# Splitting a pair's products into two calls on TensorE, with the spread as two half-height row tiles

## The chip, the cores and the metric

The kernel runs on one NeuronCore of a Trainium2 chip. The metric is the device time of one execution in microseconds (us), lower is better.

## The reference

2048 samples, each with 200 goods of 32 numbers and one candidate of 32 numbers:

```
outer  = einsum('bi,bnj->bnij', candidate, goods)           # 32*32 per item
h1     = concat(candidate, goods, outer)                    # 2048 x 200 x 1088
act    = sigmoid(h1 @ W1 + b1)                              # 36 hidden
weight = act @ W2 + b2                                      # 2048 x 200 x 1
out    = sum(goods * weight, axis=1)                        # 2048 x 32
```

## The kernel before, in words

Since the candidate is fixed within a sample, `h1 @ W1` is `goods @ Wb + bias`, where `Wb` (32 x 36) and the bias depend on the sample alone. The start of the kernel (some 24 us) makes all the `Wb` into `wm` (32 hidden units) and `wxd` (the other four) and the biases. After that the kernel runs over 64 pairs.

A unit is four samples, one in each block of 32 partitions (the block is called r). A pair is eight units, numbered by s (0 or 1) and c (0 to 3). One DMA of 800 KB brings a pair's `goods`, seven slots deep. In an iteration of the main loop TensorE works, in this order, on three different pairs:

- `products(p)`: for s, r and c one 32x32 product of 200 columns into `z_ps`, bank r, columns of s, partitions of c. The trace shows two MATMULs for each float32 product, so 64 in a call. The r-th group of s = 0 first waits until ScalarE has read bank r for pair p - 1 (`act_done`). `z_done` goes up once for each r, in the s = 1 round.
- `spread(q, 0)` and `spread(q, 1)` for q = p - 3: bf16 products with a 0/1 matrix `pick` that spread the item weights of a unit over its 128 partitions, for two units a call into one bank `s_ps[f % 2]`. Each waits for VectorE to have pooled what that bank held (`pooled`).
- `row_sums(p - 1, 0..2)`: the product with W2 into `w_ps`, 24 MATMULs with 32 columns of weights, once all of pair p - 1 is through the sigmoid (`act_done`, `actx_done`).
- `products_x(p, 0..1)`: the four other hidden units, 16 MATMULs into `x_ps`.
- `spread(q, 2)` and `spread(q, 3)`.

ScalarE does, for each r, the sigmoids of s = 0 and s = 1 (`act`, L346; waits for `z_done`, counts `act_done` once for each r) and then `actx` (L351). VectorE pools two units for each spread call (`pool_units`, L383: multiply by `goods` and sum over the 200 items), and copies `w_ps` with the bias to `whole` (`keep`, L376). GpSimd splits `whole` into three bf16 parts, which stand in `stack` (L192 to L201), and every eighth pair lays out more of `wx` (L180). Each engine works through its own list in order; semaphores tie them. The goods load of pair p waits on `pooled` for pair p - 7.

Of the kernel before, what the change touches and what calls it, by code (L numbers as in the profile page):

```python
# [10 lines left out]
P = 128  # L11
B, N, K, H = 2048, 200, 32, 36
HM = 32
# [28 lines left out]
def build(nc, goods_t, cand_r, cand_u, w1_outer, small, pick, out_t):  # L42
    with ExitStack() as ctx:  # L43
# [17 lines left out]
        pick_sb = sb("pick_sb", [P, PAIR_U, P], BF16)  # L61
# [20 lines left out]
        w2m = consts[:, C_W2M:C_W2X].rearrange("p (s m) -> p s m", s=2)  # L82
        w2x = consts[:, C_W2X:C_B2].rearrange("p (r m) -> p r m", r=4)
# [88 lines left out]
        def _(pool):  # L172
# [17 lines left out]
            for q in range(PAIRS):  # L190
# [7 lines left out]
                if q >= 2:  # L198

                    pool.wait_ge(s_done, 4 * (q - 1))  # L200
# [7 lines left out]
        def _(pe):  # L208
# [35 lines left out]
            def products(p):  # L244
                pe.wait_ge(goods_loaded[p % G_SLOTS], 16 * (p // G_SLOTS + 1))
                for s in range(2):
                    for r in range(4):
                        if s == 0 and p >= 1:

                            pe.wait_ge(act_done, 4 * (p - 1) + r + 1)  # L250
                        for c in range(4):
                            u = PAIR_U * p + 4 * s + c
                            last = nc.tensor.matmul(z_ps[32 * c:32 * c + 32, r, N * s:N * s + N],  # L253
                                                    wm[32 * r:32 * r + 32, u // RUN, :, u % RUN],
                                                    goods[32 * r:32 * r + 32, p % G_SLOTS, 4 * s + c, :],
                                                    start=True, stop=True)
                        if s == 1:
                            last.then_inc(z_done, 1)
# [15 lines left out]
            def row_sums(p, step):  # L274
                if step == 0:
                    if p >= 1:

                        pe.wait_ge(w_kept, p)
                    pe.wait_ge(act_done, 4 * p + 4)
                if step == 2:  # L280
                    pe.wait_ge(actx_done, p + 1)
                for r in range(4):
                    if step < 2:
                        left, right = w2m[:, step, :], act[:, p % A_SLOTS, r, N * step:N * step + N]
                    else:
                        left, right = w2x[:, r, :], actx[:, p % A_SLOTS, :]
                    last = nc.tensor.matmul(w_ps[32 * r:32 * r + 32, 0:N], left, right,  # L287
                                            start=step == 0, stop=step == 2)
# [3 lines left out]
            def spread(q, f):  # L292
# [4 lines left out]
                if 4 * q + f >= 2:  # L297

                    pe.wait_ge(pooled, 4 * q + f - 1)
                for i in range(2):  # L300
                    v = 2 * f + i
                    last = nc.tensor.matmul(s_ps[f % 2][:, N * i:N * i + N], pick_sb[:, v, :], stack[:, q % 2, :],  # L302
                                            start=True, stop=True)
                last.then_inc(s_done, 1)

            for p in range(PAIRS + LAG):
                q = p - LAG
                if p < PAIRS:
                    products(p)
                if q >= 0:  # L310
                    spread(q, 0)
                    spread(q, 1)
# [3 lines left out]
                if p < PAIRS:  # L316
                    products_x(p, 0)
                    products_x(p, 1)
                if q >= 0:
                    spread(q, 2)  # L320
                    spread(q, 3)

        @block.scalar
        def _(sc):
# [14 lines left out]
            for p in range(PAIRS):  # L339
# [3 lines left out]
                for r in range(4):  # L343
                    sc.wait_ge(z_done, 4 * p + r + 1)
                    for s in range(2):
                        last = nc.scalar.activation(act[:, p % A_SLOTS, r, N * s:N * s + N],  # L346
                                                    z_ps[:, r, N * s:N * s + N], ACT.Sigmoid,
                                                    bias=bias[:, r, p, s:s + 1])
                    last.then_inc(act_done, 1)
# [109 lines left out]
```

## Time and profile before

| | us |
|---|---|
| median of 3 runs | 299.07 (298.53 to 303.03) |
| the profiled execution, its time | 298.97 |
| its span, first to last instruction | 297.0 |
| TensorE busy in the span | 281.6 |
| ScalarE, VectorE, GpSimd busy | 204.3, 198.4, 195.9 |
| mean granted TensorE clock | 0.989 of full |

Busy time counts a matmul from its start to its modelled end, and overlapping matmuls once. The work of one pair repeats 64 times, so the timeline of one pair in the middle, from one `products` to the next, is the thing to read.

### The profile page before, as it was taken

Reading aid. Unit: us, or ns where it says so; the run is one execution under the profiler, and the core shown is the slowest. Engines: PE = TensorE matmul, PEld = TensorE weight load, DVE = VectorE, ACT = ScalarE, POOL = GpSimd, SP = SyncE. Lnnn points to the kernel's source line nnn. Section 1 sums busy time; section 2 is a strip of 40 time slices with the busy share of each in tenths; the row PEclk is TensorE's granted clock in tenths of the full one; section 3 lists DMA queues with packets and bytes.
Section 4 is the critical chain, followed back from the end, with each engine's and each line's share of the span. In section 5 each row is a group of like instructions: output and inputs, shape, how many; then the busy total and the mean of one; then the engine's idle time right before and its main releaser. Section 6 shows DMA issues by size and latency. Waiting matters only on the chain.

```text
span 297.0 us, 17453 instructions
## 1 busy us (share of the span) xinstructions
PE 281.6 (95%) x7480; PEld 179.6 (60%) x7480; DVE 198.4 (67%) x1109; ACT 204.3 (69%) x596; POOL 195.9 (66%) x293
## 2 busy tenths in 40 slices
PE   1997999999999999999999999999999999999983
PEld 0333666666666666666666666665666666666641
DVE  0592176766776776767767677676776767767677
ACT  2495878767777677777777877777677776777730
POOL 9900686678666876677766867676676656766663
PEclk9997999999999999999999999999999999999997
DMA  7890036556766566665666656666566765657000
GB/s 254 333 421 25 4 115 210 183 181 216 223 218 191 173 228 214 219 215 153 214 211 225 212 173 204 211 221 227 143 210 211 229 224 152 206 210 222 8 2 9
DMA packets 10588, 55.69 MB, mean 188 GB/s; under 512 B 1168, under 2 KB 1936, under 8 KB 10384
## 3 DMA queue, kind: packets, MB, share of 16 engines
q1 hardware_dynamic: 10080, 54.01, 55.3%
q8 instruction: 59, 0.97, 1.3%
q10 hardware_dynamic: 432, 0.58, 0.5%
q14 instruction: 17, 0.14, 0.2%
HBM read 54.32 MB, written 0.26 MB: 184 GB/s over the span
## 4 chain that ended last, share of the span: by engine, by line
PE 89%; ACT 4%; DVE 3%; DMA 2%; issue 1%; POOL 0%; POOLq 0%; DVEq 0%
PE z_ps L253 28%; PE w_ps L287 26%; PE s_ps L302 19%; PE x_ps L269 15%; ACT wm L337 3%; DMA act<-w_outer 2%; DVE goods L383 2%; PE z_ps L220 1%; ACT act L346 1%; DVE wxd L363 1%; PE x_ps L220 1%; POOL mid L196 0%; POOLq L43 0%; DVE bias L366 0%; DVE whole L376 0%
## 5 line engine op out<-in xcount | busy, mean ns | idle before, releaser
L346 ACT ACTIVATE act<-z_ps,bias 128x200 f32<-128x200 f32 x512 | 169.7, 443 | 69.7 <-PE z_ps L253 69.7
L383 DVE CUSTOM_DVE_ANT_0 goods<-s_ps,goods 128x200 f32<-128x200 f32 x512 | 156.5, 363 | 64.4 <-PE s_ps L302 64.4
L192 POOL TENSOR_SCALAR top<-whole,consts 128x200 bf16<-128x200 f32 x64 | 50.1, 783 | 76.7 <-DVE whole L376 76.1
L253 PE MATMUL z_ps<-goods,wm 32*32 32x200 f32 x4096 | 90.0, 357 | 1.7 <-issue 1.6
L253 PEld LDWEIGHTS z_ps<-goods,wm 32*32 32x32 f32 x4096 | 59.5, 145 | 21.1 <-issue 13.8
L302 PE MATMUL s_ps<-stack,pick_sb 128*128 128x200 bf16 x512 | 67.2, 252 | 3.2 <-DVE out_stage L383 2.6
L302 PEld LDWEIGHTS s_ps<-stack,pick_sb 128*128 128x128 bf16 x512 | 36.3, 98 | 42.7 <-issue 22.4
L287 PE MATMUL w_ps<-act,consts 128*32 128x200 f32 x1024 | 58.4, 339 | 0.7 <-issue 0.6
L269 PE MATMUL x_ps<-goods,wx 128*32 128x200 f32 x1024 | 58.0, 337 | 0.0
L196 POOL TENSOR_SCALAR mid<-rest,consts 128x200 bf16<-128x200 f32 x64 | 50.1, 782 | 6.3
L383 DVE DVE_READ_ACCUMULATOR2_ANT out_stage<- 128x1 f32 x512 | 42.8, 84 | 0.0
L376 DVE TENSOR_SCALAR whole<-w_ps,consts 128x200 f32<-128x200 f32 x64 | 27.3, 426 | 21.8 <-PE w_ps L287 15.3
L269 PEld LDWEIGHTS x_ps<-goods,wx 128*32 128x32 f32 x1024 | 34.7, 110 | 11.2 <-issue 0.9
L201 POOL TENSOR_TENSOR stack<-rest,mid 128x200 bf16<-128x200 f32 x64 | 36.4, 568 | 5.3
L194 POOL TENSOR_TENSOR rest<-whole,top 128x200 f32<-128x200 f32 x64 | 36.3, 567 | 5.3
L287 PEld LDWEIGHTS w_ps<-act,consts 128*32 128x32 f32 x1024 | 27.0, 109 | 17.0 <-issue 12.0
L287 PE MATMUL w_ps<-actx,consts 128*32 128x200 f32 x512 | 35.6, 333 | 0.5 <-issue 0.4
L351 ACT ACTIVATE actx<-x_ps,biasx 128x200 f32<-128x200 f32 x64 | 30.1, 471 | 2.3 <-PE x_ps L269 2.2
L287 PEld LDWEIGHTS w_ps<-actx,consts 128*32 128x32 f32 x512 | 17.5, 110 | 6.9 <-issue 2.0
L220 PE MATMUL z_ps<-act 32*32 32x512 f32 x160 | 10.4, 724 | 6.2 <-DMA act<-w_outer 6.2
L180 POOL COPY wx<-wxd 32x256 f32<-32x256 f32 x32 | 12.6, 394 | 2.0
L173 POOL MEMSET wx<- 128x12288 f32 x1 | 10.3, 10342 | 0.3 <-POOLq L448 0.3
(28 smaller groups left out, 56.4 us busy)
## 6 DMA issues: line engine op xcount, KB each, us to landing
goods<-goods_t SPq DMA_DIRECT2D x64, 800.0 KB, 4.4
act<-cand_r SPq DMA_DIRECT2D x1, 1024.0 KB, 5.3
act<-cand_u SPq DMA_DIRECT2D x1, 256.0 KB, 6.0
pick_sb<-pick ACTq DMA_DIRECT2D x1, 256.0 KB, 6.1
out_t<-out_stage SPq DMA_DIRECT2D x4, 64.0 KB, 4.2
consts<-small ACTq DMA_DIRECT2D x1, 164.5 KB, 6.1
act<-w_outer ACTq DMA_DIRECT2D x1, 144.0 KB, 5.4
```

The lines of the kernel that those rows point to most:

```text
L192: nc.gpsimd.tensor_scalar(top[:, :], whole[:, q % 2, :], m1, None, ALU.mult).then_inc(part_step, 1)
L194: nc.gpsimd.tensor_tensor(rest[:, :], whole[:, q % 2, :], top[:, :], ALU.subtract).then_inc(part_step, 1)
L196: nc.gpsimd.tensor_scalar(mid[:, :], rest[:, :], m2, None, ALU.mult).then_inc(part_step, 1)
L201: nc.gpsimd.tensor_tensor(stack[:, q % 2, :], rest[:, :], mid[:, :], ALU.subtract).then_inc(part_step, 1)
L253: last = nc.tensor.matmul(z_ps[32 * c:32 * c + 32, r, N * s:N * s + N], wm[32 * r:32 * r + 32, u // RUN, :, u % RUN], goods[32 * r:32 * r ...
L269: last = nc.tensor.matmul(x_ps[32 * c:32 * c + 32, 0:N], left, goods[:, p % G_SLOTS, 4 * s + c, :], start=s == 0, stop=s == 1)
L287: last = nc.tensor.matmul(w_ps[32 * r:32 * r + 32, 0:N], left, right, start=step == 0, stop=step == 2)
L302: last = nc.tensor.matmul(s_ps[f % 2][:, N * i:N * i + N], pick_sb[:, v, :], stack[:, q % 2, :], start=True, stop=True)
L346: last = nc.scalar.activation(act[:, p % A_SLOTS, r, N * s:N * s + N], z_ps[:, r, N * s:N * s + N], ACT.Sigmoid, bias=bias[:, r, p, s:s + 1])
L351: nc.scalar.activation(actx[:, p % A_SLOTS, :], x_ps[:, 0:N], ACT.Sigmoid, bias=biasx[:, p:p + 1]).then_inc(actx_done, 1)
L376: nc.vector.tensor_scalar(whole[:, p % 2, :], w_ps[:, 0:N], b2, None, ALU.add).then_inc(w_kept, 1)
L383: last = nc.vector.tensor_tensor_reduce(goods[:, q % G_SLOTS, v, :], s_ps[f % 2][:, N * i:N * i + N], goods[:, q % G_SLOTS, v, :], 1.0, 0. ...
```

## The change

`products` takes s as an argument and does one round of 32 MATMULs; each round has its own waits and its own four counts of `z_done`, so ScalarE does the four sigmoids of s = 0, then `actx`, then the four of s = 1, and counts `act_done` after each. The r-th group of round s waits for ScalarE to have read bank r of the round before it; for s = 1 that is round 0 of the same pair.

The rows of `stack` are laid out anew: the lower 64 partitions hold the item weights of the units of s = 0, the upper 64 those of s = 1. A spread call uses 64 rows for each product, with the s = 0 ones into `s_ps[0]` and the s = 1 ones into `s_ps[1]`, and does four units; there are two calls to a pair instead of four. Each waits until all four units of the call before are pooled. `pick` has half the columns. The `act` slices and weights of `row_sums` change with the layout; its count of MATMULs doesn't. The order on TensorE becomes: products(p, 0), spread(q, 0), products_x(p, 0 and 1), products(p, 1), spread(q, 1), row_sums(p - 1). The number of goods transfers and their sizes, and SyncE's code, stay as they are.

```diff
             pe.wait_ge(wb_kept[0], KEPT_ALL)
             pe.wait_ge(wb_kept[1], KEPT_ALL)
 
-            def products(p):
-                pe.wait_ge(goods_loaded[p % G_SLOTS], 16 * (p // G_SLOTS + 1))
-                for s in range(2):
-                    for r in range(4):
-                        if s == 0 and p >= 1:
-
-                            pe.wait_ge(act_done, 4 * (p - 1) + r + 1)
-                        for c in range(4):
-                            u = PAIR_U * p + 4 * s + c
-                            last = nc.tensor.matmul(z_ps[32 * c:32 * c + 32, r, N * s:N * s + N],
-                                                    wm[32 * r:32 * r + 32, u // RUN, :, u % RUN],
-                                                    goods[32 * r:32 * r + 32, p % G_SLOTS, 4 * s + c, :],
-                                                    start=True, stop=True)
-                        if s == 1:
-                            last.then_inc(z_done, 1)
+            def products(p, s):
+                if s == 0:
+                    pe.wait_ge(goods_loaded[p % G_SLOTS], 16 * (p // G_SLOTS + 1))
+                for r in range(4):
+                    if 2 * p + s >= 1:
+
+                        pe.wait_ge(act_done, 4 * (2 * p + s - 1) + r + 1)
+                    for c in range(4):
+                        u = PAIR_U * p + 4 * s + c
+                        last = nc.tensor.matmul(z_ps[32 * c:32 * c + 32, r, N * s:N * s + N],
+                                                wm[32 * r:32 * r + 32, u // RUN, :, u % RUN],
+                                                goods[32 * r:32 * r + 32, p % G_SLOTS, 4 * s + c, :],
+                                                start=True, stop=True)
+                    last.then_inc(z_done, 1)
...
-                    pe.wait_ge(act_done, 4 * p + 4)
+                    pe.wait_ge(act_done, 8 * p + 8)
                 if step == 2:
                     pe.wait_ge(actx_done, p + 1)
-                for r in range(4):
+                for t in range(4):
+
                     if step < 2:
-                        left, right = w2m[:, step, :], act[:, p % A_SLOTS, r, N * step:N * step + N]
+                        first = N * (t // 2)
+                        left, right = w2m[:, step, :], act[:, p % A_SLOTS, 2 * (t % 2) + step, first:first + N]
                     else:
-                        left, right = w2x[:, r, :], actx[:, p % A_SLOTS, :]
-                    last = nc.tensor.matmul(w_ps[32 * r:32 * r + 32, 0:N], left, right,
+                        left, right = w2x[:, t, :], actx[:, p % A_SLOTS, :]
+                    last = nc.tensor.matmul(w_ps[32 * t:32 * t + 32, 0:N], left, right,
                                             start=step == 0, stop=step == 2)
                 if step == 2:
                     last.then_inc(w_done, 1)
...
-                if 4 * q + f >= 2:
-
-                    pe.wait_ge(pooled, 4 * q + f - 1)
+                if 2 * q + f >= 1:
+
+                    pe.wait_ge(pooled, 4 * q + 2 * f)
                 for i in range(2):
-                    v = 2 * f + i
-                    last = nc.tensor.matmul(s_ps[f % 2][:, N * i:N * i + N], pick_sb[:, v, :], stack[:, q % 2, :],
-                                            start=True, stop=True)
+                    for s in range(2):
+                        rows = slice(64 * s, 64 * s + 64)
+                        last = nc.tensor.matmul(s_ps[s][:, N * i:N * i + N], pick_sb[rows, 2 * f + i, :],
+                                                stack[rows, q % 2, :], start=True, stop=True)
                 last.then_inc(s_done, 1)
 
             for p in range(PAIRS + LAG):
                 q = p - LAG
                 if p < PAIRS:
-                    products(p)
+                    products(p, 0)
                 if q >= 0:
                     spread(q, 0)
+                if p < PAIRS:
+                    products_x(p, 0)
+                    products_x(p, 1)
+                    products(p, 1)
+                if q >= 0:
                     spread(q, 1)
                 if 1 <= p <= PAIRS:
                     for step in range(3):
                         row_sums(p - 1, step)
-                if p < PAIRS:
-                    products_x(p, 0)
-                    products_x(p, 1)
-                if q >= 0:
-                    spread(q, 2)
-                    spread(q, 3)
 
...
-                for r in range(4):
-                    sc.wait_ge(z_done, 4 * p + r + 1)
-                    for s in range(2):
-                        last = nc.scalar.activation(act[:, p % A_SLOTS, r, N * s:N * s + N],
-                                                    z_ps[:, r, N * s:N * s + N], ACT.Sigmoid,
-                                                    bias=bias[:, r, p, s:s + 1])
-                    last.then_inc(act_done, 1)
-                sc.wait_ge(x_done, p + 1)
-                nc.scalar.activation(actx[:, p % A_SLOTS, :], x_ps[:, 0:N], ACT.Sigmoid,
-                                     bias=biasx[:, p:p + 1]).then_inc(actx_done, 1)
+                for s in range(2):
+                    for r in range(4):
+                        sc.wait_ge(z_done, 4 * (2 * p + s) + r + 1)
+                        nc.scalar.activation(act[:, p % A_SLOTS, r, N * s:N * s + N],
+                                             z_ps[:, r, N * s:N * s + N], ACT.Sigmoid,
+                                             bias=bias[:, r, p, s:s + 1]).then_inc(act_done, 1)
+                    if s == 0:
+                        sc.wait_ge(x_done, p + 1)
+                        nc.scalar.activation(actx[:, p % A_SLOTS, :], x_ps[:, 0:N], ACT.Sigmoid,
+                                             bias=biasx[:, p:p + 1]).then_inc(actx_done, 1)
...
-                dve.wait_ge(s_done, 4 * q + f + 1)
-                for i in range(2):
-                    v = 2 * f + i
-                    u = PAIR_U * q + v
-                    last = nc.vector.tensor_tensor_reduce(
-                        goods[:, q % G_SLOTS, v, :], s_ps[f % 2][:, N * i:N * i + N], goods[:, q % G_SLOTS, v, :],
-                        1.0, 0.0, ALU.mult, ALU.add, out_stage[:, u:u + 1])
-                last.then_inc(pooled, 1)
+                dve.wait_ge(s_done, 2 * q + f + 1)
+                for s in range(2):
+                    for i in range(2):
+                        v = 4 * s + 2 * f + i
+                        u = PAIR_U * q + v
+                        last = nc.vector.tensor_tensor_reduce(
+                            goods[:, q % G_SLOTS, v, :], s_ps[s][:, N * i:N * i + N], goods[:, q % G_SLOTS, v, :],
+                            1.0, 0.0, ALU.mult, ALU.add, out_stage[:, u:u + 1])
+                    last.then_inc(pooled, 1)
...
-                if q >= 0:
-                    pool_units(q, 2)
-                    pool_units(q, 3)
...
-    pick = np.zeros((4, 32, PAIR_U, 4, 32), mybir.dt.np(BF16))
+
+    pick = np.zeros((2, 2, 32, 4, 4, 32), mybir.dt.np(BF16))
     for r in range(4):
+        half, e = divmod(r, 2)
+        for c in range(4):
+            three = slice(12 * e + 3 * c, 12 * e + 3 * c + 3)
+            w2m[c, :, e, three] = w2[:HM, None]
+            pick[:, half, three, c, r, :] = 1.0
+            masks[:, 12 * e + 3 * c + 1:12 * e + 3 * c + 3, 0] = 1.0
+            masks[:, 12 * e + 3 * c + 2, 1] = 1.0
+            for s in range(2):
+                w2x[c, s, r, :, 2 * s + half, three] = w2[HM:, None]
```

## Rows read from the trace of the kernel before

**Rows 1.** The page: busy time, then the chain that ended last by engine.
```profile
PE 281.6 (95%) x7480; PEld 179.6 (60%) x7480; DVE 198.4 (67%) x1109; ACT 204.3 (69%) x596; POOL 195.9 (66%) x293
...
PE 89%; ACT 4%; DVE 3%; DMA 2%; issue 1%; POOL 0%; POOLq 0%; DVEq 0%
```

**Rows 2.** The page's costliest groups: ScalarE's sigmoid of the products.
```profile
L346 ACT ACTIVATE act<-z_ps,bias 128x200 f32<-128x200 f32 x512 | 169.7, 443 | 69.7 <-PE z_ps L253 69.7
```

**Rows 3.** Timeline of one pair, TensorE; start us, us, engine line op tiles xcount.
```profile
149.94 1.38 PE L253 MATMUL z_ps<-goods,wm 32*32 32x200 f32 x64
...
151.26 0.52 PE L302 MATMUL s_ps<-stack,pick_sb 128*128 128x200 bf16 x4
...
151.70 0.88 PE L287 MATMUL w_ps<-act,consts 128*32 128x200 f32 x16
...
152.74 0.86 PE L269 MATMUL x_ps<-goods,wx 128*32 128x200 f32 x16
...
153.54 0.52 PE L302 MATMUL s_ps<-stack,pick_sb 128*128 128x200 bf16 x4
...
153.99 1.37 PE L253 MATMUL z_ps<-goods,wm 32*32 32x200 f32 x64
```

**Rows 4.** Timeline, TensorE, windows up to 150.04, 150.28 and 151.30 in one products call.
```profile
149.94 0.48 PE L253 MATMUL z_ps<-goods,wm 32*32 32x200 f32 x15
...
149.94 0.65 PE L253 MATMUL z_ps<-goods,wm 32*32 32x200 f32 x32
...
150.60 0.72 PE L253 MATMUL z_ps<-goods,wm 32*32 32x200 f32 x26
```

**Rows 5.** Timeline of the same pair, ScalarE.
```profile
151.22 2.65 ACT L346 ACTIVATE act<-z_ps,bias 128x200 f32<-128x200 f32 x8 [1.06 <-PE z_ps L253]
```

**Rows 6.** Timeline of an early pair: ScalarE, then TensorE's loads and matmuls.
```profile
31.32 0.78 ACT L346 ACTIVATE act<-z_ps,bias 128x200 f32<-128x200 f32 x2
...
31.67 1.66 PE L253 MATMUL z_ps<-goods,wm 32*32 32x200 f32 x64
...
32.15 0.82 PEld L253 LDWEIGHTS z_ps<-goods,wm 32*32 32x32 f32 x40 [0.21 <-ACT act L346]
...
35.10 1.66 PE L253 MATMUL z_ps<-goods,wm 32*32 32x200 f32 x64
```

**Rows 7.** Timeline of the same pair, VectorE: pooling of four units, then keep.
```profile
151.64 0.37 DVE L383 CUSTOM_DVE_ANT_0 goods<-s_ps,goods 128x200 f32<-128x200 f32 x1 [0.53 <-PE s_ps L302]
...
152.79 0.09 DVE L383 DVE_READ_ACCUMULATOR2_ANT out_stage<- 128x1 f32 x1
153.00 0.43 DVE L376 TENSOR_SCALAR whole<-w_ps,consts 128x200 f32<-128x200 f32 x1
```

**Rows 8.** Timeline of the same pair, GpSimd: first and last part of one split.
```profile
149.48 0.78 POOL L192 TENSOR_SCALAR top<-whole,consts 128x200 bf16<-128x200 f32 x1 [1.07 <-DVE whole L376]
...
151.88 0.57 POOL L201 TENSOR_TENSOR stack<-rest,mid 128x200 bf16<-128x200 f32 x1
```

**Rows 9.** Timeline of a pair with a layout of weights on GpSimd.
```profile
129.13 1.38 PE L253 MATMUL z_ps<-goods,wm 32*32 32x200 f32 x64
...
130.88 1.36 PE L287 MATMUL w_ps<-act,consts 128*32 128x200 f32 x14
...
131.69 1.76 POOL L180 COPY wx<-wxd 32x256 f32<-32x256 f32 x4
...
133.81 1.37 PE L253 MATMUL z_ps<-goods,wm 32*32 32x200 f32 x64
```

**Rows 10.** Timeline of the end: last products, last row sums, keep, last spread.
```profile
281.77 1.37 PE L253 MATMUL z_ps<-goods,wm 32*32 32x200 f32 x64
...
287.31 0.89 PE L287 MATMUL w_ps<-act,consts 128*32 128x200 f32 x16
...
288.60 0.43 DVE L376 TENSOR_SCALAR whole<-w_ps,consts 128x200 f32<-128x200 f32 x1 [0.45 <-PE w_ps L287]
...
292.13 0.75 PE L302 MATMUL s_ps<-stack,pick_sb 128*128 128x200 bf16 x4 [0.39 <-POOL stack L201]
```

More of the change, by code:

```diff
@@ L60, in build @@
         consts = sb("consts", [P, C_ALL])
-        pick_sb = sb("pick_sb", [P, PAIR_U, P], BF16)
+        pick_sb = sb("pick_sb", [P, 4, P], BF16)
         bias = sb("bias", [P, 4, PAIRS, 2])
@@ L81, in build @@
         b1x = consts[:, C_B1X:C_W2M]
-        w2m = consts[:, C_W2M:C_W2X].rearrange("p (s m) -> p s m", s=2)
-        w2x = consts[:, C_W2X:C_B2].rearrange("p (r m) -> p r m", r=4)
+        w2m = consts[:, C_W2M:C_W2X].rearrange("p (e m) -> p e m", e=2)
+        w2x = consts[:, C_W2X:C_B2].rearrange("p (t m) -> p t m", t=4)
         b2 = consts[:, C_B2:C_M1]
@@ L198, in _ @@
                 if q >= 2:
-                    pool.wait_ge(s_done, 4 * (q - 1))
+                    pool.wait_ge(s_done, 2 * (q - 1))
                 nc.gpsimd.tensor_tensor(stack[:, q % 2, :], rest[:, :], mid[:, :], ALU.subtract).then_inc(part_step, 1)
@@ L428 @@
     masks = np.zeros((4, 32, 2), f32)
-    pick = np.zeros((4, 32, PAIR_U, 4, 32), mybir.dt.np(BF16))
+    pick = np.zeros((2, 2, 32, 4, 4, 32), mybir.dt.np(BF16))
     for r in range(4):
+        half, e = divmod(r, 2)
[7 more added lines that the diff above has]
+                w2x[c, s, r, :, 2 * s + half, three] = w2[HM:, None]
         for s in range(2):
             w1x[r, :, s, s, r, :] = w1_cand[:, HM:]
-            for c in range(4):
-                v = 4 * s + c
-                w2m[c, :, s, 3 * v:3 * v + 3] = w2[:HM, None]
-                w2x[c, s, r, :, r, 3 * v:3 * v + 3] = w2[HM:, None]
-                pick[r, 3 * v:3 * v + 3, v, r, :] = 1.0
-                masks[r, 3 * v + 1:3 * v + 3, 0] = 1.0
-                masks[r, 3 * v + 2, 1] = 1.0
     small[:, C_W1X:C_B1M] = w1x.reshape(P, 64)
@@ L450 @@
     for name, a in (("goods_t", goods_t), ("cand_r", cand_r), ("cand_u", cand_u), ("w1_outer", w1_outer),
-                    ("small", small), ("pick", pick.reshape(P, PAIR_U, P))):
+                    ("small", small), ("pick", pick.reshape(P, 4, P))):
         arrays[name] = a
```

## The prediction

> **What bounds the kernel now.** I read the page first: TensorE is busy 95% of the span, the three other engines 66 to 69%, and TensorE carries 89% of the chain that ended last [rows 1]. Then the timeline of one pair in the middle, TensorE alone. It has no gap: products 149.94 to 151.26 (1.32), two spread calls to 151.70 (0.44), row sums to 152.74 (1.04), products_x to 153.54 (0.80), two spread calls to 153.99 (0.45), and the next products [rows 3]. That is 4.04 us to a pair, 64 times 258 of the 297 us. I call such a stretch a frame and count from its first matmul. Last, what the others do in a frame. ScalarE does its eight sigmoids in 2.65 us, after it sat idle 1.06 for the products [rows 5]; that idle time is 69.7 us in all [rows 2]. Nobody waits for it: after the frame's X and S work its results are there. TensorE is the bound, ScalarE the nearest other one: nine activations at 0.317 ((2.65 - 0.43) / 7 [rows 5]) are 2.85 a pair.
>
> **The spread calls.** Before there are two blocks of four full-height matmuls, 0.44 and 0.45. After there are two blocks of four with 64 rows each. Two products of a block lie in different rows and banks. If they stream side by side, a block costs two steps instead of four. One step of 200 bf16 columns is about (0.44 - 0.10) / 4 = 0.085, where 0.10 is what a change of tile shape costs: six steps of row sums take 1.04, so 0.173 each, and the four steps of products_x, which end in such a change, take 0.80, that is 0.69 + 0.11 [rows 3]. Side by side gives 2 x 0.085 + 0.11 = 0.28. No row shows tiles of 64 rows. Bounds: 0.28 from below (the four 32-column tiles that stream together in row sums are the pattern: four matmuls in one step of 0.173), 0.44 from above, as if nothing overlapped. I take 0.28, since the 32x32 and the 128x32 tiles of this kernel do overlap: 64 matmuls of at least 0.33 us in 1.32 us.
>
> The Trainium skill's page TensorEngine Tiling (Array Packing), Key Properties, says that different tiles load and multiply in parallel, and names 64x128 as a mode with two tiles; no row here shows that mode. Taken as it stands it gives the lower of the two values.
>
> **The products in two calls.** Of the call's 64 matmuls 32 have started by 150.28 and have ended at 150.59 (0.65 from the start) [rows 4]. The whole call's last one ends by the model at 151.32, but the spread starts at 151.26 [rows 3, 4], 0.06 before that end. So a call of 32 alone costs 0.65 - 0.06 = 0.59, and two cost 1.18 where the one cost 1.32, if nothing makes them wait.
>
> **Changes of shape.** Before, row sums run straight into products_x, of the same tile shape. After, each stands alone: row sums cost 1.04 + 0.11 = 1.15, products_x 0.80 as now. Four changes to a pair become six. If TensorE never waited, the new frame would be 0.59 + 0.28 + 0.80 + 0.59 + 0.28 + 1.15 = 3.69, that is 0.35 less than 4.04. It does wait.
>
> **The new wait.** products(p, 1), group r, may only start once ScalarE has read bank r of products(p, 0), in the same frame. Now that distance is a whole frame; after the change only spread(q, 0) and products_x lie between, 0.28 + 0.80. Follow it from the frame's start:
> - First sigmoid. It starts 1.28 after the start of products now (151.22 - 149.94 [rows 3, 5]), and the counting round starts one call of 32 in, 0.59. So it starts 1.28 - 0.59 = 0.69 after a call's start.
> - The fourth sigmoid of the round ends 3 x 0.317 + 0.46 = 1.41 later (durations: 0.43 to 0.47), at 2.10.
> - TensorE goes on 0.05 after that: the sigmoid of the early pair ends at 31.32 + 0.78 = 32.10 and the loads held for it start at 32.15 [rows 6]. So group r = 3 of products(p, 1) starts at 2.15.
> - Without a wait, products(p, 1) would start at 0.59 + 0.28 + 0.80 = 1.67 and its fourth group at about 1.75 (15 of the 16 first-pass matmuls start within 0.10 [rows 4]). So it stands 0.40.
> - From the release of the fourth group to the next call: the 0.59 less the 0.08 of the three groups before it, 0.51. The end of products(p, 1) is 2.66.
> Queued behind this wait on TensorE are spread(q, 1), row_sums(p - 1) and the next products(p + 1, 0). Hence the frame is 2.66 + 0.28 + 1.15 = 4.09, against 4.04. What the first spread call saves is lost in the wait; the second's saving (0.16) and the separated calls stand against the extra shape change and the 0.4 us wait. The wait is the step on which all hangs.
>
> **The others in such a frame.** ScalarE: round 0 till 2.1, actx (its products are done at about 2.0), round 1 at about 2.35 to 3.75; the next frame needs it at 4.1. VectorE: a block of four poolings goes from 0.38 after the spread's start to 1.6 after (151.26, 151.64, 152.79 + 0.09 [rows 3, 7]). The second spread call comes 2.66 - 0.59 = 2.07 after the first and needs that; the next first call comes 2.0 later. Both have 0.4 to spare, so the wait for all four units costs nothing; without that slack each call would cost up to 0.4. GpSimd: a split lasts 2.97 (149.48 to 152.45 [rows 8]) with 1.07 idle before the next. keep comes after the second pooling, at about 4.3 of its frame, the split is done at 7.8, its spread is due two frames on at 8.18 + 0.59 = 8.8. A layout adds 1.76 [rows 9], of which 1.1 fall into idle time; 0.7 remain, and the slack is 1.0. That's covered, though barely; if not, a few tenths every eighth frame. Goods and the pick transfer: goods slots come free once a frame as now; the smaller pick is loaded long before its use. Both nothing.
>
> **Start, end, supply.** The first frames have no spread: 3.43 now (35.10 - 31.67 [rows 6]), 2.66 + 1.15 = 3.81 after, for two or three frames +1.0. At the end, now: row sums 5.5 after the last products start, keep 6.8 after (281.77, 287.31, 288.60 [rows 10]). After: the spread of pair 61 comes at 4.3, its pooling takes 1.6, its second call at 6.0, row sums at 6.3, and keep after VectorE's second block at 7.8: +1.0. The last two spread calls, one after the other, put a 0.4 us hole between the poolings, so +0.4. Some seven frames are longer than 4.04 now, such as 129.13 to 133.81, 4.68, where the row sums' matmuls themselves hang, 1.36 for 14 [rows 9]; together some 4 us by the frames' lengths in the timeline. Where they fall into the new wait they are hidden; I take off 1.0.
>
> **Sum.** The profiled execution took 298.97, its span 297.0, the median is 299.07: the same. 61 frames with spread x 0.05 = 3.0; start +1.0; end +1.4; supply -1.0. That is 298.97 + 4.4 = 303.4.
>
> **Rivals.**
> - The wait falls away. If the first sigmoid starts early enough for the fourth group not to wait, the frame is 3.69 and the time 299 - 61 x 0.35 = 277.6 plus 1.4, 279. For it: TensorE's work in a frame does shrink. Against it: the release at 2.15 is made of four sigmoids one after the other, that are seen in every frame; it would have to come at 1.75. A part of it is likelier: if the release comes 0.15 earlier, since the short call's first group finishes sooner than in the long one, the frame is 3.94 and the time 294. Together 0.15.
> - The half-height products don't stream side by side. Then the second spread call costs 0.44, the frame is 4.25, and the time 303.4 + 61 x 0.16 = 313. The first call's 0.16 vanish in the wait. For it: nothing of this shape is in the trace. Against it: the other tile shapes overlap. It decides from a block of some 0.34 on: 0.06 x 61 = 3.7 more than my sum, over the 2% line at 305.0. Chance 0.27.
> - The layouts or supply stalls break the thin covers (GpSimd 0.3, pooling 0.4): each eighth frame 0.5 to 1 longer, +4 to +8, 307 to 311. Chance 0.10.
> - As forecast: 0.48, between 299 and 307. Of that 0.10 lie above 305.
>
> **Range and chances.** 2% is about what this measurement tells from no change: 293.1 to 305.0. The range goes from 294 (the partly relieved wait) to 313 (no overlap). Faster by over 2%: 0.13, nearly all of the first rival. Slower: 0.27 and 0.09 of the next two and 0.10 of the forecast, 0.46. Within: 0.38 of the forecast and 0.03 from the first and third rival, 0.41. The forecast is the likeliest single case, but its time stands just inside the line.
>
> **What would show it.** In the profile after: frames of 4.09; the fourth group's loads of products(p, 1) held by ScalarE's activate, idle 0.3 to 0.4 before them, released 2.15 into the frame; the four matmuls of a spread in two steps, 0.28 to the next block; ScalarE's idle time in two pieces, before each round. I am wrong if the release comes before 1.8, if the spread takes 0.44, or if the loads of a spread call are held by VectorE or GpSimd.

## The result and the profile after

The changed kernel takes 303.47 us (median of 13 runs, 300.09 to 304.20) against 299.13 us before (13 runs, 298.19 to 303.03). The ratio is 1.009, interval 1.005 to 1.013: slower by about 1%, on the near side of 2%. The medians lie 4.3 us apart, the means of the same 13 executions each 2.6 us (302.6 and 300.0). The forecast was 303.4.

The page of the changed kernel, for its span, busy time, chain and ScalarE's sigmoids; its profiled execution took 303.67 us:

```profile
span 301.7 us, 17453 instructions
...
PE 281.9 (93%) x7480; PEld 147.2 (49%) x7480; DVE 195.4 (65%) x1109; ACT 207.6 (69%) x596; POOL 195.9 (65%) x293
...
PE 86%; DVE 4%; ACT 3%; POOL 2%; issue 2%; DMA 2%; POOLq 0%; DVEq 0%
...
L347 ACT ACTIVATE act<-z_ps,bias 128x200 f32<-128x200 f32 x512 | 177.2, 428 | 68.7 <-PE z_ps L253 68.1
```

Busy time has hardly moved against [rows 1, 2]: 281.9 against 281.6 us of TensorE, and ScalarE still waits 68 us for the products. The page alone would say that nothing happened. The frame says what did. This is the timeline of one pair, all engines, one row for each call (start us, us, engine, line, operation, tiles, count):

```profile
152.20 0.67 PE L253 MATMUL z_ps<-goods,wm 32*32 32x200 f32 x32
...
152.80 0.35 PE L304 MATMUL s_ps<-stack,pick_sb 64*128 64x200 bf16 x4
...
152.90 1.38 ACT L347 ACTIVATE act<-z_ps,bias 128x200 f32<-128x200 f32 x4 [1.06 <-PE z_ps L253]
...
153.07 0.89 PE L268 MATMUL x_ps<-goods,wx 128*32 128x200 f32 x16
153.19 0.37 DVE L385 CUSTOM_DVE_ANT_0 goods<-s_ps,goods 128x200 f32<-128x200 f32 x1 [0.42 <-PE s_ps L304]
...
153.89 1.01 PE L253 MATMUL z_ps<-goods,wm 32*32 32x200 f32 x32
...
154.15 0.45 ACT L352 ACTIVATE actx<-x_ps,biasx 128x200 f32<-128x200 f32 x1
...
154.83 0.35 PE L304 MATMUL s_ps<-stack,pick_sb 64*128 64x200 bf16 x4
...
155.11 0.89 PE L288 MATMUL w_ps<-act,consts 128*32 128x200 f32 x16
...
156.26 0.67 PE L253 MATMUL z_ps<-goods,wm 32*32 32x200 f32 x32
```

From 152.20 to 156.26 it is 4.06 us, where it was 4.04 [rows 3]. Reading down: the first products call and its change to the spread cost 0.60, the spread 0.27 (0.44 before), products_x 0.82, the second products call 0.94, the spread 0.28, the row sums 1.15. The two products calls do the same work, yet the first runs 0.67 by the modelled ends and the second 1.01. Why is seen in a narrow window on TensorE's weight loads:

```profile
154.33 0.21 PEld L253 LDWEIGHTS z_ps<-goods,wm 32*32 32x32 f32 x8
```

These are the eight loads of the fourth group of the second call. They start at 154.33, 0.44 after that call's start and 2.13 after the frame's. ScalarE's four sigmoids of round 0 run from 152.90 to 154.28, and the loads go 0.05 after that. VectorE (153.19, 0.42 idle before it) isn't late for anybody here. It is so in nearly every frame; this is what TensorE's loads waited for from 40 to 270 us, some 56 frames (engine, line, releaser: us in total, times, longest us):

```profile
PEld z_ps L253 <- ACT act L347: 18.2, 56, 0.6
...
PEld s_ps L304 <- POOL stack L201: 1.7, 5, 0.5
PEld s_ps L304 <- DVE out_stage L385: 0.3, 1, 0.3
```

That is 0.33 us to a frame for ScalarE, and single cases for GpSimd and VectorE.

The rest of the difference lies outside the usual frames. Frames are counted between starts of a pair's first products call: pair 0, pair 4 and pair 63 start at 24.12, 39.41 and 281.77 before and at 24.73, 41.36 and 284.78 after. So, in the two profiled executions:

| stretch | before | after | difference |
|---|---|---|---|
| up to pair 0 | 24.12 | 24.73 | +0.6 |
| pairs 0 to 4 | 15.29 | 16.63 | +1.3 |
| pairs 4 to 63, 59 frames | 242.36 | 243.42 | +1.1 |
| from pair 63 to the end | 15.20 | 16.89 | +1.7 |
| span | 297.0 | 301.7 | +4.7 |

In the third row 59 frames of the usual length, 4.037 and 4.071 (the median frame of each), make 238.2 and 240.2: +2.0 by the frame itself. What is left, 4.2 and 3.2 us, are single longer frames: -1.0. Below, the long frames of a kernel are always this: the time from pair 4 to pair 63 less 59 times its median frame, in one execution.

The first two rows hold something that isn't the kernel's. Near the start TensorE's clock stands at its lower level for a while, in these two executions until 27.6 us before and 32.3 us after. Here are the same 4 us, first of the kernel before and then of the one after (us, busy us of PE, PEld, DVE, ACT, POOL with counts, granted clock, DMA share, GB/s):

```profile
28.00:32.00 4.00, 3.94 (x121) 2.39 (x112) 0.43 (x1) 3.56 (x13) 0.24 (x1) 1.00 0.02 4
```

```profile
28.00:32.00 4.00, 3.72 (x80) 1.83 (x80) 0.00 (x0) 2.86 (x9) 0.00 (x0) 0.50 0.00 0
```

After, the stretch from 28 to 32 runs at 0.50 of the clock, that is 1.2 GHz; before, it ran at 2.4. But this changes from one execution to the next. Two of the experiments below leave out the goods loads from pair 7 on, and up to there they are the kernel before and the changed kernel unaltered. The same window of theirs, first the kernel before and then the changed one:

```profile
28.00:32.00 4.00, 4.00 (x83) 2.10 (x72) 0.00 (x0) 3.23 (x11) 0.00 (x0) 0.50 0.01 4
```

```profile
28.00:32.00 4.00, 3.96 (x107) 2.36 (x107) 0.00 (x0) 3.69 (x12) 0.00 (x0) 1.00 0.02 4
```

Now it is the kernel before that stands at the lower clock (until 33.9 us), and the changed one doesn't (it is back at 27.5). In this execution of the changed kernel pair 0 starts at 24.10, pairs 0 to 4 take 15.68 and the end takes 16.61. Against the profile before (24.12, 15.29 and 15.20), whose clock rose as early, that is nothing, +0.4 and +1.4. With +2.0 for the frame and -1.0 for the long frames the change itself is then worth some +2.8 us; the rest of the 4.7 goes with the clock of the two executions that were profiled. The times say the same. Of the 48 executions of the kernel before that ran beside the experiments, 24 had a mean granted clock of 0.987 or more (median 298.7 us) and 8 one under 0.98 (median 300.9); of the 13 of the changed kernel it was 1 (300.5) and 8 (303.65). Whether the changed kernel meets the long stretch more often isn't settled: without the loads it was 7 of 10 with less than 0.987 for the changed kernel, and 8 of 9 for the kernel before.

The end, by the last products and the last three spread calls of the changed kernel:

```profile
284.78 0.66 PE L253 MATMUL z_ps<-goods,wm 32*32 32x200 f32 x32
...
294.30 0.34 PE L304 MATMUL s_ps<-stack,pick_sb 64*128 64x200 bf16 x4 [1.33 <-DVE out_stage L385]
296.07 0.52 PE L304 MATMUL s_ps<-stack,pick_sb 64*128 64x200 bf16 x4 [1.42 <-DVE out_stage L385]
297.92 0.51 PE L304 MATMUL s_ps<-stack,pick_sb 64*128 64x200 bf16 x4 [1.33 <-DVE out_stage L385]
```

Each spread call waits for four poolings: 1.8 us from call to call, as nothing else is left to do in between.

### The profile page after: what moved, and what is told of

Read it like the earlier page. It is cut to its first block, busy times and chain, and to the rows that moved or that the text cites. A ratio compares the mean times of both kernels' runs of the same rounds, so it can differ in the third digit from the quotient of the medians.

```text
span 301.7 us, 17453 instructions
## 1 busy us (share of the span) xinstructions
PE 281.9 (93%) x7480; PEld 147.2 (49%) x7480; DVE 195.4 (65%) x1109; ACT 207.6 (69%) x596; POOL 195.9 (65%) x293
## 4 chain that ended last, share of the span: by engine, by line
PE 86%; DVE 4%; ACT 3%; POOL 2%; issue 2%; DMA 2%; POOLq 0%; DVEq 0%
PE z_ps L253 32%; PE w_ps L288 23%; PE x_ps L268 18%; PE s_ps L304 12%; ACT wm L338 3%; DVE goods L385 3%; DMA act<-w_outer 2%; PE z_ps L220 1%; DVE wxd L364 1%; PE x_ps L220 1%; POOL wx L180 1%; POOL top L192 1%; POOL mid L196 1%; POOL rest L194 0%; POOL stack L201 0%
## 5 line engine op out<-in xcount | busy, mean ns | idle before, releaser
L347 ACT ACTIVATE act<-z_ps,bias 128x200 f32<-128x200 f32 x512 | 177.2, 428 | 68.7 <-PE z_ps L253 68.1
L253 PE MATMUL z_ps<-goods,wm 32*32 32x200 f32 x4096 | 109.6, 360 | 3.0 <-issue 2.4
L253 PEld LDWEIGHTS z_ps<-goods,wm 32*32 32x32 f32 x4096 | 55.3, 146 | 53.3 <-issue 27.2
L268 PE MATMUL x_ps<-goods,wx 128*32 128x200 f32 x1024 | 58.9, 345 | 0.7 <-issue 0.7
L288 PE MATMUL w_ps<-act,consts 128*32 128x200 f32 x1024 | 56.7, 339 | 0.0
L304 PE MATMUL s_ps<-stack,pick_sb 64*128 64x200 bf16 x512 | 44.6, 253 | 6.1 <-DVE out_stage L385 5.9
L268 PEld LDWEIGHTS x_ps<-goods,wx 128*32 128x32 f32 x1024 | 27.3, 110 | 18.1 <-issue 12.5
L304 PEld LDWEIGHTS s_ps<-stack,pick_sb 64*128 64x128 bf16 x512 | 14.7, 94 | 42.8 <-issue 33.7
L288 PE MATMUL w_ps<-actx,consts 128*32 128x200 f32 x512 | 33.4, 332 | 0.0
L352 ACT ACTIVATE actx<-x_ps,biasx 128x200 f32<-128x200 f32 x64 | 28.5, 445 | 2.1 <-PE x_ps L268 2.0
```

The source lines that it names most:

```text
L268: last = nc.tensor.matmul(x_ps[32 * c:32 * c + 32, 0:N], left, goods[:, p % G_SLOTS, 4 * s + c, :], start=s == 0, stop=s == 1)
L288: last = nc.tensor.matmul(w_ps[32 * t:32 * t + 32, 0:N], left, right, start=step == 0, stop=step == 2)
L304: last = nc.tensor.matmul(s_ps[s][:, N * i:N * i + N], pick_sb[rows, 2 * f + i, :], stack[rows, q % 2, :], start=True, stop=True)
L352: nc.scalar.activation(actx[:, p % A_SLOTS, :], x_ps[:, 0:N], ACT.Sigmoid, bias=biasx[:, p:p + 1]).then_inc(actx_done, 1)
```

## The experiments

Ten kernels in three groups; the kernel before ran beside each group, with medians of 299.31, 299.53 and 299.96. The diffs show TensorE's list or the line that matters; where TensorE's order changes, the waits and the lists of the other engines follow it.

**The two halves of the change, each alone.** First the spread half: `products(p)` whole, the new layout and the two half-height calls.

```diff
-                    products(p, 0)
+                    products(p)
                 if q >= 0:
                     spread(q, 0)
-                if p < PAIRS:
-                    products_x(p, 0)
-                    products_x(p, 1)
-                    products(p, 1)
-                if q >= 0:
-                    spread(q, 1)
                 if 1 <= p <= PAIRS:
                     for step in range(3):
                         row_sums(p - 1, step)
+                if p < PAIRS:
+                    products_x(p, 0)
+                    products_x(p, 1)
+                if q >= 0:
+                    spread(q, 1)
```

> Half of the change alone: the half-height spread in two calls and the new layout of stack, with products(p) whole in one call as before. Order: products, spread 0, row sums, products_x, spread 1. My theory (the spread saves, the split with its wait gives it back): frame 1.32 + 0.28 + 1.04 + 0.80 + 0.28 = 3.72, and 0.05 to 0.1 more where VectorE's four poolings (1.65 with their wait) or ScalarE's last group (3.9 after the products' start) just miss; 61 frames less 0.25 to 0.3: 282 to 286 us. Rival, the half-height spread brings nothing by itself (waits for its single buffered banks): 299.

Measured: 297.3 us (294.5 to 301.4, 10 runs), ratio 0.990 (0.986 to 0.994). It is faster, as expected, but by 2 us and not by 13 to 17. One frame:

```profile
152.31 0.35 PE L305 MATMUL s_ps<-stack,pick_sb 64*128 64x200 bf16 x4
...
152.58 1.37 PE L253 MATMUL z_ps<-goods,wm 32*32 32x200 f32 x64
152.70 0.37 DVE L385 CUSTOM_DVE_ANT_0 goods<-s_ps,goods 128x200 f32<-128x200 f32 x1 [0.51 <-PE s_ps L305]
...
153.85 2.65 ACT L347 ACTIVATE act<-z_ps,bias 128x200 f32<-128x200 f32 x8 [0.91 <-PE z_ps L253]
...
154.08 0.35 PE L305 MATMUL s_ps<-stack,pick_sb 64*128 64x200 bf16 x4
...
156.19 0.34 PE L305 MATMUL s_ps<-stack,pick_sb 64*128 64x200 bf16 x4
...
156.47 1.37 PE L253 MATMUL z_ps<-goods,wm 32*32 32x200 f32 x64
```

From spread to spread it is 156.19 - 152.31 = 3.88, not 3.72. The products call now holds the spread back: 152.58 to 154.08 is 1.50, where it was 1.32. The first spread call of a pair waits for VectorE's four poolings of the second (152.70 to 153.94), 1.77 us from one call to the next, where I had put 1.65. That's 0.16 a frame. The rest is in single long frames, of a kind that no semaphore explains:

```profile
128.91 0.24 PE L305 MATMUL s_ps<-stack,pick_sb 64*128 64x200 bf16 x1
...
130.14 0.33 PE L305 MATMUL s_ps<-stack,pick_sb 64*128 64x200 bf16 x3 [0.99 <-issue]
```

One matmul of a spread call runs, and the other three start 1.2 us later. Such frames add 11.0 us over the usual length past pair 4 (11.2 in the expectations below, by a frame rounded to 3.88), against 4.2 before and 3.2 after the change. (This profiled execution took 301.4 us, 4 above the median of its kernel, so its sums are high ones.) The experiments without goods traffic take them up. The end is 2.7 us longer than before, 17.9 from the last products call on against 15.2: there each spread call waits for the poolings of the one before. And pairs 0 to 4 took 17.2 against 15.3, with the clock low until 33.8 us: that is this execution's.

Then the products half alone, with the full-height spread in four calls:

```diff
-                    products(p)
+                    products(p, 0)
                 if q >= 0:
                     spread(q, 0)
                     spread(q, 1)
-                if 1 <= p <= PAIRS:
-                    for step in range(3):
-                        row_sums(p - 1, step)
                 if p < PAIRS:
                     products_x(p, 0)
                     products_x(p, 1)
+                    products(p, 1)
                 if q >= 0:
                     spread(q, 2)
                     spread(q, 3)
+                if 1 <= p <= PAIRS:
+                    for step in range(3):
+                        row_sums(p - 1, step)
```

> The other half alone: products in two calls, the full-height spread in four calls as before, the order products 0, spread 0 and 1, products_x, products 1, spread 2 and 3, row sums. My theory: the fourth group of products 1 is released 2.15 into the frame, the call ends at 2.66, then 0.44 for the spread and 1.15 for the row sums, frame 4.25, so 299 + 61 x 0.21 + 1 = 313 us. Rival, the split costs nothing and only the changed end and start made the changed kernel slower: 299 to 300.

Measured: 311.54 us (309.4 to 312.0), ratio 1.038 (1.032 to 1.044). Its frames in the middle are 4.25 long (153.09 to 157.34, from first products call to first products call), the expected number. So one half gives and the other takes. Frame by frame the half-height spread is worth 0.16 without the split (4.04 to 3.88) and 0.18 with it (4.25 to 4.07). Some 60 frames of 0.16 are 9.6 us; alone it gains 2, as the long frames and the end take most of that back.

**One activation more, in two places.** In the first kernel it stands ahead of ScalarE's fourth sigmoid of round 0, in the second at the end of ScalarE's frame.

```diff
+                        if s == 0 and r == 3:
+                            nc.scalar.activation(junk[:, 0, :], consts[:, 0:N], ACT.Sigmoid)
                         sc.wait_ge(z_done, 4 * (2 * p + s) + r + 1)
```

> The changed kernel with one activation more in each frame, 200 columns from one SBUF tensor to another that nobody reads, put ahead of ScalarE's fourth sigmoid of round 0. ScalarE is idle 68.7 us of the span. My theory, the chain products 0, four sigmoids, fourth group of products 1 sets the frame: every frame grows by the whole 0.31, 64 x 0.31 = 20 us, 323 us. Rival, TensorE's own work sets it and ScalarE has room: 303.5.

> The changed kernel with the same extra activation as in the run with it ahead of the fourth sigmoid, but at the end of ScalarE's frame, after round 1. ScalarE's load is the same as there. My theory: round 1's results are awaited with some 0.3 to spare and the extra 0.26 fits into ScalarE's idle time, 303.5 within 1. Rival, ScalarE's load as such costs: 317 as there.

Measured: 316.96 us (315.7 to 318.2), ratio 1.057 (1.051 to 1.064), for the first; 302.72 us (301.9 to 303.7), ratio 1.011 (1.006 to 1.017), for the second. The same work costs 14 us in one place and nothing in the other. The first kernel's timeline, ScalarE and TensorE:

```profile
150.16 0.66 PE L254 MATMUL z_ps<-goods,wm 32*32 32x200 f32 x32
...
150.86 1.06 ACT L350 ACTIVATE act<-z_ps,bias 128x200 f32<-128x200 f32 x3 [1.10 <-PE z_ps L254]
...
151.81 0.38 ACT L348 ACTIVATE junk<-consts 128x200 f32<-128x200 f32 x1
...
151.84 1.28 PE L254 MATMUL z_ps<-goods,wm 32*32 32x200 f32 x32
...
152.07 0.43 ACT L350 ACTIVATE act<-z_ps,bias 128x200 f32<-128x200 f32 x1
...
152.55 0.22 PEld L254 LDWEIGHTS z_ps<-goods,wm 32*32 32x32 f32 x8 [0.36 <-ACT act L350]
...
154.48 0.67 PE L254 MATMUL z_ps<-goods,wm 32*32 32x200 f32 x32
```

The extra activation takes a slot of 0.26 (151.81 to 152.07), not 0.31, and the frame is 154.48 - 150.16 = 4.32, also 0.26 longer. The loads at 152.55 are the eight of the fourth group, now 2.39 after the frame's start instead of 2.13: again 0.05 after the fourth sigmoid, which ends at 152.50. The chain that was argued is the one that sets the frame; ScalarE's load is not. The time was to be 323: 3.2 of the 6 us that are missing are the smaller slot (64 x 0.05), and 2.7 are long frames, which sum to 0.5 here and to 3.2 in the changed kernel.

**Round 0 made short.** Most of round 0's activations are left out:

```diff
+                        n = N if s == 1 or p < A_SLOTS else 8
-                        nc.scalar.activation(act[:, p % A_SLOTS, r, N * s:N * s + N],
-                                             z_ps[:, r, N * s:N * s + N], ACT.Sigmoid,
+                        nc.scalar.activation(act[:, p % A_SLOTS, r, N * s:N * s + n],
+                                             z_ps[:, r, N * s:N * s + n], ACT.Sigmoid,
```

> The changed kernel with round 0's sigmoids cut to 8 of 200 columns from the fourth pair on (the rest of act keeps old values, so most of that round's activations are left out). TensorE's work is the same. My theory: the fourth group of products 1 no longer waits, the frame is TensorE's sum 3.7, 303.5 - 61 x 0.37 = 281 us. Rival, the frame is set by TensorE's changes of tile shape or by the spread: 303.

Measured: 289.70 us (288.8 to 291.6), ratio 0.967 (0.962 to 0.973).

```profile
150.96 0.66 PE L253 MATMUL z_ps<-goods,wm 32*32 32x200 f32 x32
...
151.67 0.74 ACT L348 ACTIVATE act<-z_ps,bias 128x8 f32<-128x8 f32 x4 [0.70 <-PE z_ps L253]
...
152.65 0.67 PE L253 MATMUL z_ps<-goods,wm 32*32 32x200 f32 x32
...
154.69 0.67 PE L253 MATMUL z_ps<-goods,wm 32*32 32x200 f32 x32
```

Both products calls now run 0.67, and the frame is 154.69 - 150.96 = 3.73, the sum of TensorE's own work (3.69 was forecast). So the wait was all that stood between 4.07 and 3.73. That the time is 290 and not 281 is mostly the long frames again, 9.4 us past pair 4 where the changed kernel has 3.2; some 2 more are the frame, 0.34 shorter and not 0.37.

**Row sums between the calls in place of products_x.**

```diff
                 if q >= 0:
                     spread(q, 0)
-                if p < PAIRS:
-                    products_x(p, 0)
-                    products_x(p, 1)
-                    products(p, 1)
-                if q >= 0:
-                    spread(q, 1)
                 if 1 <= p <= PAIRS:
                     for step in range(3):
                         row_sums(p - 1, step)
+                if p < PAIRS:
+                    products(p, 1)
+                if q >= 0:
+                    spread(q, 1)
+                if p < PAIRS:
+                    products_x(p, 0)
+                    products_x(p, 1)
```

> The changed kernel with row sums and products_x in each other's place: products 0, spread 0, row sums, products 1, spread 1, products_x (actx after round 1 on ScalarE, keep between the two poolings on VectorE). My theory: a call's fourth group can't start sooner than 2.13 after the start of the call before it, whichever half of the frame is shorter waits. Now the second half, 0.59 + 0.28 + 0.80 = 1.67, is the short one: the wait of 0.35 moves to products 0, products 1 takes 0.60, the frame stays 4.07, 303 to 304 us. Rival, the place was unlucky and row sums between the calls would hide the wait: frame 3.75, 284 to 290 us.

Measured: 302.17 us (299.9 to 303.0), ratio 1.008 (1.005 to 1.012). TensorE's products calls:

```profile
149.88 0.96 PE L253 MATMUL z_ps<-goods,wm 32*32 32x200 f32 x32
...
152.20 0.67 PE L253 MATMUL z_ps<-goods,wm 32*32 32x200 f32 x32
...
153.89 0.97 PE L253 MATMUL z_ps<-goods,wm 32*32 32x200 f32 x32
```

The first call of the frame is now the long one (0.96) and the second the short one (0.67): the wait moved to the other call and the total stayed. The frame is 4.01, 0.06 less than forecast; the first sigmoid of the round that now matters starts 0.64 after its call, not 0.70. I take that to be the second wait (for `w_done`) that ScalarE has only before round 0, which isn't tested. The bound is thus not a place in the order but the time from a call's start to the fourth group of the next, 2.13 us. For no wait at all both halves of a frame would have to last 2.05 (2.13 less the 0.08 that the three groups before it take), 4.1 together, and TensorE has work for 3.7.

**The spread half with its first call moved.**

```diff
+                if 1 <= p <= PAIRS:
+                    row_sums(p - 1, 0)
                 if q >= 0:
                     spread(q, 0)
                 if 1 <= p <= PAIRS:
-                    for step in range(3):
-                        row_sums(p - 1, step)
+                    row_sums(p - 1, 1)
+                    row_sums(p - 1, 2)
```

> The kernel with the half-height spread and whole products, with the first spread call moved behind the first step of row sums. In that kernel the first call stood 0.16 to 0.19 for VectorE's poolings of the second (1.74 from one call to the next, 1.60 of work). My theory: the distance becomes 2.0 and 1.85, the wait goes, one change of shape (0.11) comes, frame 3.83 against 3.88: 3 us less, 294 us. Rival, VectorE's wait isn't what holds that call: frame 3.99, 304.

Measured: 291.32 us (289.9 to 294.0, 6 runs), ratio 0.974 (0.969 to 0.980). TensorE's calls:

```profile
152.54 0.35 PE L305 MATMUL s_ps<-stack,pick_sb 64*128 64x200 bf16 x4
152.81 1.37 PE L253 MATMUL z_ps<-goods,wm 32*32 32x200 f32 x64
154.11 0.55 PE L289 MATMUL w_ps<-act,consts 128*32 128x200 f32 x8
154.59 0.35 PE L305 MATMUL s_ps<-stack,pick_sb 64*128 64x200 bf16 x4
...
156.63 1.38 PE L253 MATMUL z_ps<-goods,wm 32*32 32x200 f32 x64
```

The frame is 156.63 - 152.81 = 3.82, as forecast, and the distances between spread calls are 2.05 (152.54 to 154.59) and 1.77 (154.59 to 156.36). It beats both kernels. Against the kernel it was made from it is 6 us faster rather than 3; its long frames sum to 4.9 us past pair 4, not 11.0.

**Without the goods traffic.** In three kernels the loads of the last 57 pairs are left out:

```diff
+                if p < G_SLOTS:
                     sp.dma_start(goods[:, p % G_SLOTS, :, :].rearrange("p u n -> p (u n)"),
```

> The kernel with the half-height spread and whole products, without the goods transfers after the first seven (the slots are worked over again, so the loads of 57 pairs are left out). That kernel's 13.9 us of frames beyond 3.88 hold stretches in which TensorE issues nothing and no semaphore holds it. If the fetching of TensorE's instructions, 59 transfers of 16 KB, is slowed by the goods traffic, these stretches shrink: 288 to 291 us. If they come from the instruction stream itself, they stay: 297.

> The kernel before without the goods transfers after the first seven, as was done to the kernel with the half-height spread alone (loads of 57 pairs left out). There the frames beyond the usual length went from 11.2 us to 0.8 past the fourth pair. Here they are 4.3 us. If the goods traffic is what lengthens them here too, 299.5 - 4 = 295.5 us; if not, 299.5.

> The changed kernel without the same transfers (loads of 57 pairs left out). Its frames beyond 4.07 sum to 3.0 us past the fourth pair. If the traffic makes them, 303.0 - 3 = 300 us, and the changed kernel stays 4 to 5 us behind the one before treated alike, which is the part that its own frame (60 x 0.035), start and end carry. If the changed kernel lost by the traffic alone, both are equal.

Measured: the spread half 290.27 us (289.9 to 291.8), 7.0 less than with its traffic; the kernel before 296.75 (294.8 to 297.8), 3.2 less than the kernel before beside it; the changed kernel 301.01 (298.8 to 302.0), some 2.5 less than with its traffic. The long frames past pair 4 shrink to 0.8, 0.0 and 0.3 us: in the last two, 59 frames last 238.20 and 240.60, 4.037 and 4.078 each. So the long frames come with the goods traffic. The order of the two kernels doesn't hang on them: 4.3 us lie between the medians with no traffic, as with it.

The traces also tell what TensorE lacks in the gaps. Its instructions come in 59 transfers of 16 KB, and the traces with all loads have 15,163 instructions of TensorE, 257 to a transfer. Take the gaps of 0.48 us and more between two weight loads, from pair 4 to pair 63. In the spread half there are ten, of 0.5 to 1.9 us, beside one of 0.6 that recurs in nearly each frame. Counted from TensorE's first instruction, all ten end 193 to 195 past a multiple of 256, and 1.43 to 1.63 us after such a transfer has ended. So do the four in the kernel before (193 or 194, 1.38 to 1.46 us) and seven of the eight in the changed one (193 or 194, 1.23 to 1.46 us). This says that the gaps are waits for the next instructions. How the traffic makes them isn't shown: the transfers themselves are no longer with it (median 0.95 us in the spread half, 1.11 without loads), so it would be their start that comes late, and no run changed that alone.

## Why the prediction was right

**The main step held by itself, and the sum as a whole, the latter in part by luck.** The first sigmoid was to start 0.69 into the frame: 0.70 (152.90 - 152.20). The fourth group was to be released at 2.15: 2.13. The fourth group was to stand 0.40: the second call takes 0.94 instead of 0.60, so 0.34. Two products calls of 0.59 if nothing waits: 0.60 and, with round 0 cut short, 0.60 again. The half-height spread at 0.28: 0.27 to 0.28. Row sums at 1.15: 1.15. The frame was to be 4.09 and is 4.07. The step that decides the direction, the wait, was tested from both sides: a longer chain lengthens the frame by its own length, a shorter one frees it down to 3.73, and the same load elsewhere does nothing.

**The rivals.** Products not streaming side by side is out: the four matmuls of a spread take 0.35 by their modelled ends (0.52 before), 0.28 to the next call. In a call of the middle the four start at 0, 3, 96 and 100 ns, two by two; at full height they start at 0, 97, 183 and 269 ns. The Trainium skill's page TensorEngine Tiling (Array Packing) says under Key Properties that tiles load and multiply in parallel, and names 64x128 under Available Configurations. The trace agrees, now with a row of this shape. The wait falling away is out as well, and would have been worth 0.34 a frame. The thin covers held: in 56 frames the loads of the spread waited five times for GpSimd and once for VectorE, 2.0 us in all. One limit was misplaced: with 1.6 us between 303.4 and the 2% line, the rival without overlap decides from a block of 0.31 on (0.28 + 1.6 / 61), and not from 0.34.

**Terms that were off and cancelled.** The frame was taken 0.02 too long: 61 x 0.05 = 3.0 forecast, 2.0 measured. The start was forecast +1.0. The two profiled executions differ there by +1.3, and by another 0.6 ahead of pair 0, but most of that is the clock, which rose later in one execution than in the other; where it rose alike it is +0.4. The end was forecast +1.4 and is +1.7, or +1.4 where the clock rose alike. The supply term, -1.0, was right in size (-1.0, one execution of each). Its reason, that stalls hide in the new wait, wasn't tested alone; the list at the end speaks for it. The forecast counted 4.4 for the change. The medians lie 4.3 apart and the two profiles 4.7, but both hold clock that the prediction had no term for, and without it the change is worth some 2.8 (2.6 by the means). The direction and the wait were foreseen; that the number came out within 0.1 us is luck.

**What the prediction didn't ask.** It took the two halves as one. Alone, the spread half is worth 2 us as it was written and 8 with one call moved, and the split costs 12. The forecast sentence that the first spread call's saving is lost in the wait is the reason why the changed kernel could not win; had I summed the frame without the split, I would have seen a faster kernel next to the one that I was given. That sum would have been too good as well: the expectation for the spread half missed by some 12 us, by the frame (3.88 for 3.72 to 3.8: VectorE's round trip is 1.77, not 1.65), the end (2.7) and the long frames.

## What to carry to other kernels

When one pass over a buffer is cut in two, the distance between the engine that fills it and the one that empties it shrinks by half, while the round trip does not: here 0.7 us to the first sigmoid and 1.4 for four, against 1.69 us between the two calls. Before cutting, compare that round trip with the work that lies between, for both halves; the one that falls short waits, and it doesn't help to change which. An engine that idles 68 us can still set the time by what it does first.

Two steps that save and lose should be timed apart. The half that was hidden here is worth 2.6%, once one of its calls is moved.

## What the runs showed that was not expected

- TensorE has issue gaps without a semaphore that go away with the goods traffic: 4.2 us of long frames past pair 4 with it and 0.0 without in the kernel before, 11.0 and 0.8 in the one with the spread half. They end at the same count past a multiple of 256 instructions, 1.2 to 1.6 us after a transfer of TensorE's instructions. With the wait for ScalarE in each frame the sum is smaller (0.5 with the extra activation at 4.33 a frame, 0.7 with the split alone, 2.9, 3.2 and 3.5 in the three others), without that wait larger (4.2 in the kernel before, 4.9, 9.4 and 11.0). Each is from one execution, and what sets its size isn't settled.
- The time at the lower clock near the start differs between executions of the same code: until 27.6 and until 33.9 us for the kernel before. It is a part of the spread between runs, and two single profiles can differ by it.
- A spread call to the next one that overwrites its banks takes at least 1.77 us when four units have to be pooled in between: 0.39 to VectorE's start, 1.24 for four poolings, and 0.14 back.
- The extra activation takes a slot of 0.26 us where the sigmoid of the same 200 columns takes 0.31. It reads SBUF and has no bias from memory, the other reads PSUM and has one; which of the two counts wasn't tried.
